# Four modulated convolutions folded into one: another split of a two-column product, with its shared part copied by ScalarE inside PSUM

## The reference

```
for i, typ in enumerate(('same', 'upsample', 'same', 'downsample')):
    s = style @ mod_w[i].T + mod_b[i]
    weight = SCALE * weights[i] * s[:, None, :, None]          # 64 x 64 x 3 for each sample
    weight = weight * rsqrt(sum(weight**2, axis=(2, 3)) + EPS)
    out = conv of that type (blur by [1,3,3,1] behind 'upsample', ahead of 'downsample') + bias
return x + out
```

## Time and profile before

| | us |
|---|---|
| median of 3 runs (lowest, highest) | 758.87 (758.21, 759.43) |
| the profiled execution, and its span | 758.99, 757.2 |
| busy PE, DVE, POOL, ACT | 651.7, 599.4, 551.6, 384.0 |

### The profile page before, as it was taken

The page is one execution under the profiler, slowest core; times in us unless marked ns, Lnnn a source line. Parts: engine busy times, 40 slices in busy tenths (PEclk is TensorE's granted clock), DMA queues, the critical chain, the costliest instruction groups (busy, mean ns, idle before and its releaser), DMA issues.

```text
span 757.2 us, 13802 instructions
## 1 busy us (share of the span) xinstructions
PE 651.7 (86%) x5010; PEld 635.1 (84%) x5010; DVE 599.4 (79%) x776; ACT 384.0 (51%) x597; POOL 551.6 (73%) x524
## 2 busy tenths in 40 slices
PE   5558989799798998889898898989899898989876
PEld 4557989799798998889898898989889798988876
DVE  6984797878789787877978787897878788887863
ACT  3334555355555555555554566545456555535542
POOL 3435788786787988687797888868787888878522
PEclk9968999899999999999999999989999999999999
DMA  6055477677576767656577777746777667757762
GB/s 224 1 118 137 125 185 180 155 176 200 140 184 161 187 171 202 175 148 179 155 186 171 181 197 176 177 143 176 168 176 200 155 185 180 184 134 200 178 174 98
DMA packets 146115, 125.72 MB, mean 166 GB/s; under 512 B 5568, under 2 KB 112448, under 8 KB 146048
## 3 DMA queue, kind: packets, MB, share of 16 engines
q1 hardware_dynamic: 145392, 123.27, 63.5%
q10 hardware_dynamic: 656, 1.57, 0.6%
HBM read 36.47 MB, written 33.82 MB: 93 GB/s over the span
## 4 chain that ended last, share of the span: by engine, by line
PE 53%; DVE 27%; POOL 8%; issue 6%; ACT 4%; DMA 0%; DVEq 0%; POOLq 0%; ACTq 0%
PE pb L171 8%; DVE xl L674 7%; PE pb L172 7%; PE pb L173 7%; PE ps L171 6%; POOL Q2l L582 5%; PE ps L173 5%; PE ps L172 5%; PE pg L171 4%; PE pg L173 3%; PE pg L172 3%; DVE Gf L692 2%; DVE T L729 2%; DVE Wf L711 2%; POOL Q2h L180 2%
## 5 line engine op out<-in xcount | busy, mean ns | idle before, releaser
L171 PE MATMUL pb<-xh,W 128*128 128x256 f32 x640 | 187.3, 293 | 16.0 <-ACT AB L447 16.0
L172 PE MATMUL pb<-xl,W 128*128 128x256 f32 x640 | 185.3, 290 | 0.0
L173 PE MATMUL pb<-xh,W 128*128 128x256 f32 x640 | 184.2, 288 | 0.0
L171 PE MATMUL ps<-xh,W 128*128 128x256 f32 x384 | 114.7, 299 | 53.4 <-DVE xl L674 51.2
L171 PEld LDWEIGHTS pb<-xh,W 128*128 128x128 f32 x640 | 129.7, 203 | 19.6 <-ACT AB L447 19.6
L618 POOL TENSOR_TENSOR T<-AB 128x256 f32<-128x256 f32 x128 | 95.1, 743 | 60.5 <-issue 33.4
L729 DVE SCALAR_TENSOR_TENSOR T<-pb,DD,AB 128x256 f32<-128x256 f32 x128 | 61.2, 478 | 98.4 <-PE pb L173 77.3
L442 ACT ACTIVATE AB<-ps,cv,DD 128x256 f32<-128x256 f32 x128 | 71.9, 562 | 126.8 <-PE ps L173 126.8
L172 PEld LDWEIGHTS pb<-xl,W 128*128 128x128 f32 x640 | 129.6, 202 | 0.0
L173 PEld LDWEIGHTS pb<-xh,W 128*128 128x128 f32 x640 | 129.4, 202 | 0.0
L171 PEld LDWEIGHTS ps<-xh,W 128*128 128x128 f32 x384 | 77.5, 202 | 60.7 <-issue 60.7
(11 more groups left out here) (169 smaller groups left out, 1726.9 us busy)
## 6 DMA issues: line engine op xcount, KB each, us to landing
X<-in_xin SPq DMA_DIRECT2D x64, 516.0 KB, 5.0
out<-T SPq DMA_DIRECT2D x64, 512.0 KB, 3.3
W<-W SPq DMA_DIRECT2D x64, 384.0 KB, 5.7
W<-W SPq DMA_DIRECT2D x32, 512.0 KB, 6.4
W<-M SPq DMA_DIRECT2D x64, 128.0 KB, 6.7
W<-W SPq DMA_DIRECT2D x32, 128.0 KB, 4.4
E<-in_ed ACTq DMA_DIRECT2D x1, 768.0 KB, 7.2
XE<-in_xe SPq DMA_DIRECT2D x1, 576.0 KB, 4.6
```

The costliest lines, as they stand in the source:

```text
L171: eng.matmul(o, wh_, rh, start=first, stop=False, skip_group_check=onto)
L172: eng.matmul(o, wh_, rl, start=False, stop=False, skip_group_check=onto)
L173: return eng.matmul(o, wl_, rh, start=False, stop=last, skip_group_check=onto)
```

## The change

One product is now shared by both results: conv_shared gives S = (W0+W1) O(k) + (W2+W3) O(k+1) + W4 O(k+2). With x parts 2 = E(k) - O(k) and 3 = E(k+1) - O(k) (POOL makes two subtractions a pair instead of one), conv_rest adds W0, W2, W4 times part 2 for the even and W1, W3 times part 3 for the odd results. It has again eight tap products: nine matmuls in conv_shared, fifteen in conv_rest.

ACT copies S from its bank into both halves of a result bank (shared_copy into py, two banks), PE adds the rest onto it there, and ACT takes both halves out at once, with scale and bias, into T (result, two samples later). a_out, b_out, even_out, odd_out and AB go. Two matmuls ahead of the loop write the py banks once. SP's stores wait for `result` in place of DVE and POOL.

Q2 and G are no longer moved to SBUF in float32: `full` scales them in place in PSUM, ACT's `high` reads them there, and `low` is DVE's, reading PSUM. A unit's bank is therefore free for reuse four units on only after `low`, not after `full`. The scaling of Q3 (q3_full) goes from POOL to ACT, as four instructions. w_diff becomes w_sum (three additions of 256 columns or fewer), the tap parts are cast and subtracted as 768, 768 and 256 columns, w_low of the parts 1 and 2 goes to the next sample, and `cross` has nine DMAs and 1792 KB. xh and xl have three buffers instead of two. In the diff a line of "..." stands for what is left out; removed functions can be read above.

```diff
-XH = 2
+XH = 3
 TR = 2
-AR = 3
+YR = 2
 NP = 4
-NX = 6
+NX = 9
...
+S0, W0, W1, S2, W2, W3, W4 = range(7)
+PARTS = [slice(S0, W1 + 1), slice(S2, W3 + 1)]
+
+XO, XE0, XO1 = range(3)
...
-        pb = [psum("pb0"), psum("pb1")]
         pg = [psum(f"pg{i}") for i in range(NP)]
         pe_ = psum("pe")
+        py = [psum(f"py{i}") for i in range(YR)]
         ps = psum("ps")
-        pa = ps[:, 0:H]
+        pm = ps[:, 0:H]
...
+                if k == 0:
+                    sp.dma_start(w[hi, S0:W1 + 1, :, :, 1], w[lo, S0:W1 + 1, :, :, 0]).then_inc(s_w[g % 2], 16)
+                    sp.dma_start(w[lo, S0, :, :, 1], w[hi, W0, :, :, 0]).then_inc(s_w[g % 2], 16)
+                    sp.dma_start(w[lo, W1, :, :, 1], w[hi, W0, :, :, 0]).then_inc(s_w[g % 2], 16)
+                elif k == 1:
+                    sp.dma_start(w[hi, S2:W3 + 1, :, :, 1], w[lo, S2:W3 + 1, :, :, 0]).then_inc(s_w[g % 2], 16)
+                    sp.dma_start(w[lo, W2, :, :, 1], w[hi, W1, :, :, 0]).then_inc(s_w[g % 2], 16)
+                    sp.dma_start(w[lo, W3:W4 + 1, :, :, 1], w[hi, W2:W3 + 1, :, :, 0]).then_inc(s_w[g % 2], 16)
+                else:
+                    sp.dma_start(w[lo, W4, :, :, 0], r32(M[lo])).then_inc(s_w[g % 2], 16)
+                    sp.dma_start(w[hi, W4, :, :, 1], r32(M[lo])).then_inc(s_w[g % 2], 16)
+                    sp.dma_start(w[lo, S2, :, :, 1], r32(M[hi])).then_inc(s_w[g % 2], 16)
...
+                taps(b, pm, XO, ((S0, True, False), (S2, False, False), (W4, False, True))).then_inc(s_a, 1)
+
+            def conv_rest(b):
+                pe.wait_ge(s_ae, b + 1)
+                o = py[b % YR]
+                taps(b, o[:, H:2 * H], XO1, ((W1, False, False), (W3, False, True)), True)
+                taps(b, o[:, 0:H], XE0, ((W0, False, False), (W2, False, False), (W4, False, True)), True).then_inc(s_p, 1)
 
             def unit(g, u):
                 n = PLACE[g, u]
                 o = [bank(pg[n % NP], 1)[:, :, 0]] if u in (1, 6) else [bank(pg[n % NP], 2)[:, :, v] for v in range(2)]
                 if n >= NP:
-                    pe.wait_ge(s_ce, n - NP + 1)
+                    h, v = ORDER[n - NP]
+                    if v < 2:
+                        pe.wait_ge(s_q2l, 2 * h + v + 1)
+                    elif v < 4:
+                        pe.wait_ge(s_gl, 3 * h + 2 * v - 3)
+                    else:
+                        pe.wait_ge(s_ce, n - NP + 1)
...
+            for i in range(YR):
+                pe.matmul(py[i][:, :], A2h[:, 0:128], A2h[:, :], start=True, stop=True)
...
-                conv_even(b)
+                conv_shared(b)
                 if b:
-                    conv_diff(b - 1)
-                conv_odd(b)
+                    conv_rest(b - 1)
...
-                act.copy(xh[:, n % XH], X[:, n % XR]).then_inc(s_xh, 1)
-
-            def a_out(b):
+                act.copy(xh[:, n % XH], X[:, n % XR, :, 1:4]).then_inc(s_xh, 1)
+
+            def shared_copy(b):
                 act.wait_ge(s_a, b + 1)
...
+                if b >= YR:
+                    act.wait_ge(s_y, b - YR + 1)
+                act.copy(py[b % YR][:, :].rearrange("p (e k) -> p e k", e=2),
+                         pm.unsqueeze(1).to_broadcast([128, 2, H])).then_inc(s_ae, 1)
+
+            def result(b):
+                n, q = divmod(b, Q)
+                act.wait_ge(s_p, b + 1)
+                if q == 0 and n >= TR:
+                    act.wait_ge(s_st[n % TR], 16 * (n // TR))
+                act.activation(T[:, n % TR, q].rearrange("p e k -> p (e k)"), py[b % YR][:, :], ACT.Identity,
+                               bias=cv[:, b:b + 1], scale=DD[:, 3, b:b + 1]).then_inc(s_y, 1)
+
+            def q3_full(g):
+                act.wait_ge(s_q3h, g)
+                act.wait_ge(s_q3l, 2 * g)
+                for i in range(NG):
+                    m = act.mul(Q3f[:, i // 2].rearrange("p v (o b) -> p v o b", b=2)[:, :, :, i % 2], q3s[:],
+                                D32[:, g * NG + i:g * NG + i + 1])
+                m.then_inc(s_q3f, 1)
...
+                k = 1 if u == 1 else 2
+                src = bank(pg[PLACE[g, u] % NP], k)
                 if u < 2:
-                    v = slice(0, 2) if u == 0 else slice(2, 3)
                     if g:
                         act.wait_ge(s_c, cnt(g - 1, 3))
-                    act.copy(Q2h[:, :, v], Q2f[:, :, v]).then_inc(s_q2h, 1)
-                else:
-                    v = slice(0, 2) if u == 2 else slice(2, 4)
+                    act.copy(Q2h[:, :, 2 * u:2 * u + k], src).then_inc(s_q2h, 1)
+                else:
                     if g:
                         act.wait_ge(s_c, cnt(g - 1, 6))
-                    act.copy(Gh[:, :, v], Gf[:, :, v]).then_inc(s_gh, 1)
+                    act.copy(Gh[:, :, 2 * u - 4:2 * u - 2], src).then_inc(s_gh, 1)
...
-                act.wait_ge(s_cd, 2 * g + min(k, 1) + 1)
                 if k < 2:
+                    act.wait_ge(s_cd, 2 * g + k + 1)
                     if g >= 2:
                         act.wait_ge(s_p, NG * (g - 1))
                     act.copy(taps_of(g, 0, k), Wf[:, :, PARTS[k]]).then_inc(s_wh, 1)
                 else:
+                    act.wait_ge(s_ce, cnt(g, 6))
                     if g:
                         act.wait_ge(s_w[(g - 1) % 2], 16 * NX * ((g - 1) // 2 + 1))
-                    act.copy(outer_of(0), Wf[hi, :, OUTER]).then_inc(s_wh, 1)
+                    act.copy(M[:, 0], Wf[:, :, W4]).then_inc(s_wh, 1)
...
-                if b:
-                    b_out(b - 1)
+                if b >= 2:
+                    result(b - 2)
                 else:
                     act.wait_ge(s_sc, SC_CV)
-                n = (b + 1) // Q
-                if b % Q == 1 and XH <= n < NQ:
+                if b == 0:
+                    q3_full(3)
+                n = b // Q + 1
+                if b % Q == 0 and 2 <= n < NQ:
                     x_high(n)
+                for x in units_of(b):
+                    if x[1] == 4:
+                        w_high(x[0], 0)
+                    elif x[1] < 4:
+                        high(*x)
+                shared_copy(b)
+                for x in units_of(b):
+                    if x[1] == 4:
+                        w_high(x[0], 1)
+                        w_high(x[0], 2)
                 if i == 1 and g + 3 < NGR:
                     q3_high(g + 3)
...
+                if i == 3 and g + 4 < NGR:
+                    q3_full(g + 4)
+            result(B - 2)
+            result(B - 1)
...
+                pool.tensor_tensor(x[:, :, 3, 0:XW - 1], x[:, :, 0, 1:XW], x[:, :, 1, 0:XW - 1], ALU.subtract)
+                pool.tensor_tensor(x[:, :, 2], x[:, :, 0], x[:, :, 1], ALU.subtract).then_inc(s_s, 1)
...
                 n = PLACE[g, u]
                 dve.wait_ge(s_c, n + 1)
-                src = pg[n % NP]
+                k = 1 if u in (1, 6) else 2
+                src = cols(bank(pg[n % NP], k))
                 if u < 2:
...
+                    m = tt(src, src, bc2(gs(D21, g), k), ALU.mult)
                 elif u < 4:
...
+                    m = tt(src, src, bc2(gs(D10c, g), k), ALU.mult)
+                elif u < 6:
                     if g:
                         dve.wait_ge(s_wh, 3 * g)
-                    v = {4: slice(W0, W1 + 1), 5: slice(W2, W3 + 1), 6: slice(W4, W4 + 1)}[u]
-                    k = 1 if u == 6 else 2
-                    m = tt(cols(Wf[:, :, v]), cols(bank(src, k)), bc2(gs(S[:, 0], g), k), ALU.mult)
+                        dve.wait_ge(s_wl, 3 * g)
+                    v = slice(W0, W1 + 1) if u == 4 else slice(W2, W3 + 1)
+                    m = tt(cols(Wf[:, :, v]), src, bc2(gs(S[:, 0], g), k), ALU.mult)
                     if u == 5:
                         link(m)
                         dve.wait_ge(s_id, g + 1)
                         m = tt(Wf[lo, :, W2], Wf[lo, :, W2], ID[lo], ALU.add)
+                else:
+                    dve.wait_ge(s_cd, 2 * g + 2)
+                    m = tt(cols(Wf[lo, :, W4:W4 + 1]), cols(bank(pg[n % NP], 1)[lo]), bc2(gs(S[lo, 0], g), k), ALU.mult)
                 m.then_inc(s_ce, 1)
 
-            def w_diff(g, k):
+            def low(g, u):
+                k = 1 if u == 1 else 2
+                src = bank(pg[PLACE[g, u] % NP], k)
+                if u == 0:
+                    dve.wait_ge(s_q2h, 2 * g + 1)
+                    tt(Q2l[:], src, r32(Q2h[:, :, 0:2]), ALU.subtract).then_inc(s_q2l, 1)
+                elif u == 1:
+                    dve.wait_ge(s_q2h, 2 * g + 2)
+                    lone_low(dve, Q2h[hi, :, 2], src[hi, :, 0]).then_inc(s_q2l, 1)
+                elif u == 2:
+                    dve.wait_ge(s_gh, 2 * g + 1)
+                    tt(Gl[:, :, 0:2], src, r32(Gh[:, :, 0:2]), ALU.subtract).then_inc(s_gl, 1)
+                else:
+                    dve.wait_ge(s_gh, 2 * g + 2)
+                    tt(Gl[:, :, 2], src[:, :, 0], r32(Gh[:, :, 2]), ALU.subtract).then_inc(s_gl, 1)
```

(75 more changed lines are left out.)

140 lines of the change are left out of this document (20 added, 120 removed).

## The result

The changed kernel takes 686.27 us (median of 4 runs, 686.14 to 687.51) against 758.59 for the kernel before: ratio 0.9049, 95% interval 0.9033 to 0.9065. Forecast were 726 us, range 702 to 752: the direction was right, the gain more than twice the forecast one (72 us, not 33). The profiled execution spans 684.4 us, the one before 757.2.

What follows compares the result with a forecast made beforehand. The bound was taken to be a round through PE, ACT and DVE, each working in order. Groups at 21.0 against 22.0 us (-28), with start and end terms, gave -32.5 on 759.0: 726 us, range 702 to 752.

Steps and rivals of the forecast that it cites:

- The chain behind U: PE, ACT and DVE operations after a group's start: third sample starts at 8.95 us, fourth at 13.0.
- U: Start of a group's first convolution on PE, from which times are counted; U' is the next group's start.
- PE's wait of 0.2 for the copy: PE has unit 2 until 4.56 us, ACT's shared_copy ends at 4.65, so PE waits 0.2.
- my slope: ACT's shared_copy priced at 0.470 us for 256 columns plus 256 more at the casts' 0.84 ns: 0.69 us.
- Odd groups: U' = 16.5 + E: Odd groups on PE and DVE alone: next start at 23.4 us in group 11; other steps 19.2, 21.6, 20.5.
- E: Edge step on DVE in odd groups: 6.9 us in group 11; steps 0, 2, 3 at 2.7, 5.1, 4.0.
- SP: landing at U + 20.5: Cross DMAs queue behind SP's store; first issue 7.2, plus 12.6, plus 0.7 for added bytes; next conv_shared waits for them.
- the rival of the hidden landing: Taps' landing holds up no group: 20.4 us a group, 708 us, or 700 with E shortened; chance 0.27.
- The sum: Even groups 20.5 us, odd 21.5, both 21.0 against 22.0; with start and end terms -32.5 in all.
- PE's floors of 18.6 and 19.7: PE's matmul count with hand-overs: 18.6 us in odd groups, 19.7 in even ones with PE's edge step.
- ACT was no bound: Rival that ACT bounds: copy and result take 1.0 to 1.12 us, 21.6 a group, 744 us; chance 0.10.
- the taps were not late: Rival that taps come too late: landing at U + 22.4 gives 770 us, at 23.3 gives 798; chance 0.13.

Runs made afterwards that it cites:

- c2_pool: Changed kernel with five idle POOL additions of 256 columns in the third sample of odd groups, behind POOL's own work; 717.13 us, ratio 0.9446.
- d_bytes: Changed kernel with two more 128 KB transfers of the same form ahead of each group's nine cross DMAs; 707.17 us, ratio 0.9323.
- a_psum: Kernel before with only Q2 and G scaled in place in PSUM and their low parts made by DVE, not POOL; 738.67 us, ratio 0.9743.
- e_order: Changed kernel with the first six cross DMAs of a group issued ahead of the store, the last three behind; 684.2 us, ratio 0.9014.
- ef: Changed kernel with six cross DMAs ahead of the store and edge steps 1 and 2 cut in two; 667.92 us, ratio 0.8804.
- f_split: Changed kernel with DVE's edge steps 1 and 2 cut in two, the second half moved to the next even group; 674.38 us, ratio 0.8874.
- b_conv: Changed kernel with Q2 and G scaled into SBUF, low parts on POOL as before, and two buffers of xh and xl; 720.51 us, ratio 0.9502.
- c_pool: Changed kernel with two idle POOL additions a sample, four in a group's third and fourth; 781.85 us, ratio 1.0308.

## Why the prediction was wrong, step by step

- *The chain behind U* was right in order and nearly in size. PE's wait of 0.2 for the copy did not come: the second sample starts at U + 4.57, and PE was to be free at 4.56. Third sample 8.95 against 8.71, first cross DMA 7.2 against 6.73. The copy is 0.1 us shorter than forecast, and ACT's back-to-back operations start some 0.1 before the one ahead ends, which the sum left out. The Trainium skill's figure for the copy (0.57, VectorE: DVE Perf Modes, section on the TRN2 errata) was nearer than my slope; the trace has 0.594.
- *Odd groups: U' = 16.5 + E* failed by E, and this is the first step that was mis-sized. I took E from the trace of a kernel whose POOL was busy beside DVE, 6.9 us for step 1, wrote of the quieter POOL only that it relieves DVE's operations with two SBUF operands, and priced even that at nothing in the forecast. E is 4.9 there, and 1.7, 3.6 and 2.3 in steps 0, 2 and 3, where I had 2.7, 5.1 and 4.0; the operations that shrank most (798 to 320 and 927 to 403 ns) have one SBUF operand. With E = 4.9 the same formula gives 21.4, and 20.7 was measured in group 11, since DVE also enters the step 0.9 earlier (U + 11.98 against 12.85). When c2_pool puts the traffic back, the odd groups come to 18.6, 23.7, 21.5, 19.9, where I had forecast 19.2, 23.4, 21.6 and 20.5 without the landing.
- *SP: landing at U + 20.5* is the second. The mechanism is real (d_bytes), the term was 2.0 us too long in group 11, where the taps landed at U + 18.5. The first issue gives 0.5 of it. Another 1.0 was misread in the old trace: I took 12.6 us from the first cross DMA to the last landing, with the 6.7 us that are the median of line 229 over all groups and both its copies; in group 11 the last copy took 5.5, so the time was 11.6 (11.9 on average over groups 1 to 28). The last 0.5 is the price of the added bytes: 0.7 forecast, and 0.2 measured (11.8 now; the average is 11.7, less than before). A 512 B piece occupies an engine for 35.6 ns on average, against 38.3 before. The 412 GB/s of the earlier trace rows that I set beside these copies belong to packets of 2048 and 2064 B, none of them a piece of a cross DMA, so no run here shows what longer pieces would do between two places in SBUF. So the case that came nearest is the rival of the hidden landing (0.27), which I gave 708, and 700 with a shorter E: still 14 too high.
- *The sum.* Even groups were forecast at 20.5 and took 19.9; odd ones 21.5 and took 19.4. The mean is 1.33 us a group below the forecast, 37 of the 40 us by which 726 was too high. Put the measured E into my formula, keep PE's floors of 18.6 and 19.7 and let the landing be hidden, and the odd groups come to 18.6, 21.4, 20.1, 18.8, the even ones to 19.7, the mean to 19.7. That is 759 - 28 x 2.3 - 6 = 689 us: the two mis-sized terms account for nearly all of the miss. Start, first and last groups were forecast at -4.5 us in all and gave -7.2.
- *Rivals.* ACT was no bound (425 us, 480 forecast) and the taps were not late. The range ended at 702, although one rival in my own text, the hidden landing with a shorter E, stood at 700; it had no chance of its own.

What stays open: why a piece of the cross DMAs is faster. It is 38.5 ns in a_psum, with the old six DMAs and a quieter POOL, 35.6 to 35.8 with the nine and three buffers, 35.0 in e_order and ef, where six of the nine go ahead of the store, and 33.0 to 33.2 in both kernels with nine and two buffers. So a quiet POOL alone does not do it, and placing W first did not move it. Sizes, order and neighbours of the DMAs were not varied one by one.

## What to carry to other kernels

A duration read from a trace holds for the company it was measured in. When a change empties POOL, lay POOL's timeline beside each DVE operation on the path and see whether the two end together. The fastest of one group is not enough: in the kernel before all eight operations of 192 columns take 0.79 us or more, but one of the same kind with 320 columns takes 0.38:

```profile
L765 DVE TENSOR_SCALAR HH<-AA,BB x8: 379/776/1269, 184.1 to 712.7; 64x320 f32<-64x320 f32 x8
```

When several floors lie within a microsecond or two of each other, work out the case in which two of them give way together, and let the range reach it. And take a landing from the transfer that ends last, not from a median over several. A long serial side step on an engine in order (here the edge steps) is worth cutting in pieces over several periods once it is the longest path: f_split's edit alone gave 12 us, and 18 with the earlier DMAs, but on the kernel before the same edit gave 6.

## What the runs showed of the hardware

- DVE's TENSOR_SCALAR on 64 partitions, 192 columns, takes 0.32 us where no POOL instruction runs beside it (after, a_psum, ef) and 0.80 (before), 0.88 (c2_pool), 1.02 (b_conv, c_pool) where one does; in group 11 of the kernel before each of the four ends 0.12 to 0.13 us behind the POOL instruction beside it. An addition with two SBUF operands (416 columns) goes from 0.59 to 1.11 us in c2_pool. DVE's operations of 512 columns that read PSUM stayed at 0.68 to 0.70 in every kernel, c_pool with POOL busy for 607 us included.
- ACT's copy of 512 columns from PSUM to PSUM takes 0.594 us, and its casts of 512 columns 0.589 from PSUM, 0.622 from SBUF.
- Idle work of 355 us on POOL (c_pool) cost the changed kernel 96 us, and 80 additions placed beside the edge steps (c2_pool) 31; in both, part of that is time at half clock (some 96 and 49 us of the run, against 25).
- In group 11 of the changed kernel PE waits 2.12 us, and its granted clock is 0.50 from 294.2 to 297.4, behind the wait.
